# Where the first layer's gate rows are normalised: six of eight groups on GpSimd instead of ScalarE

## The reference, cut to what matters

```
x = x + attn_a(layernorm(x))     # arccos-kernel attention against 512 keys
x = x + ffn(layernorm(x))        # first layer: gate, top 2 of 8 experts, plus a shared expert
x = x + attn_b(layernorm(x))     # linear attention
x = x + ffn(layernorm(x))        # second layer
```

## Time and profile before

| what | us |
|---|---|
| median of 3 runs | 753.15 (751.16 to 757.9) |
| the profiled execution, its time | 754.43 |
| its span in the profile | 752.7 |
| mean granted TensorE clock, share of full speed | 0.89 |
| busy VectorE / TensorE / ScalarE / GpSimd | 551.8 / 523.5 / 425.5 / 379.0 |
| window 100 to 150 us: VectorE / ScalarE / GpSimd busy | 38.93 / 46.24 / 11.79 |
| window 150 to 200 us: VectorE / ScalarE / GpSimd busy | 37.98 / 28.34 / 23.06 |

### The profile page before, as it was taken

How to read it: one execution, slowest core, us unless ns; L and a number is a source line. 1 busy time by engine, 2 the same in 40 slices (tenths; PEclk the granted TensorE clock), 3 DMA queues, 4 the chain that set the end, 5 groups by cost and what they waited for, 6 DMA issues and landing times.

```text
span 752.7 us, 15794 instructions
## 1 busy us (share of the span) xinstructions
PE 523.5 (70%) x4441; PEld 376.2 (50%) x4442; DVE 551.8 (73%) x1219; ACT 425.5 (57%) x781; POOL 379.0 (50%) x374
## 2 busy tenths in 40 slices
PE   1376725564469949999993577764699689999940
PEld 0132225563224327788882466653244367888830
DVE  4987677888679818788882478875978377888835
ACT  1289988993446516566660468744455276666610
POOL 4032103233777744778875112246777426668760
PEclk9999969887689979999997689977699899999985
DMA  9600000000111313443432310000113134343319
GB/s 282 178 0 0 1 0 1 0 1 15 43 46 54 96 49 70 84 92 88 91 75 84 123 56 2 1 23 32 48 50 103 47 69 88 85 88 88 79 51 330
DMA packets 95049, 51.10 MB, mean 68 GB/s; under 512 B 76026, under 2 KB 84180, under 8 KB 94996
## 3 DMA queue, kind: packets, MB, share of 16 engines
q1 hardware_dynamic: 85908, 31.67, 17.3%
q0 software_dynamic: 9088, 18.76, 7.9%
HBM read 16.27 MB, written 23.90 MB: 53 GB/s over the span
## 4 chain that ended last, share of the span: by engine, by line
PE 36%; DVE 18%; POOL 14%; issue 14%; ACT 7%; DMA 6%; SPq 4%; POOLq 0%; DVEq 0%; ACTq 0%
POOL routed_rows L660 12%; PE PC L1218 6%; PE PC L1016 4%; PE PC L1220 4%; PE PC L1219 4%; PE PA L1202 3%; PE PA L1203 2%; PE PA L1204 2%; DMA big<-routed_rows 2%; DVE BN L1238 2%; SPq L526 2%; DMA RR<-expert_results 2%; PE PA L995 1%; DVE big L1443 1%; PE PB L1202 1%
## 5 line engine op out<-in xcount | busy, mean ns | idle before, releaser
L716 POOL DMA_INDIRECT expert_results<-RR,DG x156 | 176.2, 1130 | 96.3 <-DVE RR L1795 54.1
L660 POOL DMA_INDIRECT routed_rows<-big,SLQ x128 | 137.3, 1073 | 55.7 <-issue 44.8
L951 ACT ACTIVATE SC<-PA,B1T,scl 128x256 f32<-128x256 f32 x208 | 100.5, 564 | 77.3 <-PE PA L1204 77.3
L1218 PE MATMUL PC<-W2H,big 128*128 x624 | 118.4, 222 | 5.1 <-issue 3.0
L1219 PE MATMUL PC<-W2H,big 128*128 x624 | 116.7, 219 | 0.0
L1220 PE MATMUL PC<-W2L,big 128*128 x624 | 116.6, 219 | 0.0
L1786 DVE SCALAR_TENSOR_TENSOR big<-SC,scl,big 128x1024 f16<-128x1024 f32 x78 | 100.2, 1284 | 2.8
L1218 PEld LDWEIGHTS PC<-W2H,big 128*128 128x128 f16 x624 | 60.5, 97 | 26.8 <-issue 17.5
L1202 PE MATMUL PA<-big,W1H 128*128 128x256 f16 x208 | 59.1, 284 | 18.7 <-DMA big<-routed_rows 17.2
L1016 PE MATMUL PC<-QW,big 128*128 128x128 f32 x256 | 41.1, 336 | 42.6 <-DVE big L1443 27.9
L607 POOL TENSOR_TENSOR RS<-VA,halfneg 128x4 f32<-128x4 f32 x24 | 28.0, 1168 | 82.0 <-DVE VA L1477 81.9
(11 more groups left out here) (271 smaller groups left out, 1254.8 us busy)
## 6 DMA issues: line engine op xcount, KB each, us to landing
RR<-expert_results SPq DMA_DIRECT2D x16, 512.0 KB, 4.3
routed_rows<-pad_zeros SPq DMA_DIRECT2D x23, 128.0 KB
expert_results<-RR,DG POOLq DMA_INDIRECT x156
X<-n_L_attn_a_hidden_states SPq DMA_DIRECT2D x2, 1024.0 KB, 6.8
big<-in_L_ffn_w SPq DMA_DIRECT2D x1, 2048.0 KB, 8.9
routed_rows<-big,SLQ POOLq DMA_INDIRECT x128, 2.4
out_x<-X SPq DMA_DIRECT2D x8, 256.0 KB, 5.4
big<-routed_rows SPq DMA_TRANSPOSE x78
```

What stands on the lines that cost most here:

```text
L660: pool.indirect_dma_start(routed, bass.IndirectOffsetOnAxis(ap=SLQ[:, slot, t, c:c + 1], axis=0), XHL[:, slot, t, c, :].bitcast(I32), None ...
L716: pool.indirect_dma_start(results, bass.IndirectOffsetOnAxis(ap=DG[:, k, r, 0:1], axis=0), YT[:, k, r, :], None).then_inc(result_stored[k] ...
L951: ins = act.activation(HF[:, k % 3, b * RU:(b + 1) * RU], up_out(k, b), ACT.Gelu, scale=INV1, bias=B1T[:, bass.ds(b1_at + b, 1)])
L1218: pe.matmul(o, hh, W2H[:, at], start=(b == 0), stop=False)
```

## The change

For groups 0 to 5 of the first layer GpSimd makes the normalised rows: after the root of the group it computes (X - mean) times root for each of the four tiles. ScalarE's four instructions and VectorE's shift for these groups go. VectorE's `first_hi` waits for GpSimd's semaphore in place of ScalarE's. Groups 6 and 7, and the second layer, keep ScalarE's form, with the counts of their semaphores lowered by six.

```
+    POOLED = NG - 2
...
+            def normalise(g):
+
+                pool.wait_ge(s["root_made"], norm_turn[1, g] + 1)
+                wait(pool, s["xl_ready"], g - 1)
+                for t in range(TPG):
+                    at = g * TPG + t
+                    last = pool.tensor_scalar(XNG[:, g % 2, t, :], X[:, at, :], MV[:, at, 0:1], RS[:, at:at + 1],
+                                              ALU.subtract, ALU.mult)
+                last.then_inc(s["p_xn"], 1)
...
                     for g in range(NG - 2):
                         x_scale(g)
                         group_root(g, 1)
+                        normalise(g)
...
                     def first_normalise(g):
-                        gate_normalise(g)
+                        if g >= POOLED:
+                            gate_normalise(g)
                         if g == NG // 2 + 1:
                             gap(0)
...
                 def first_shift(g):
-                    shift(g, 1)
+                    if g >= POOLED:
+                        shift(g, 1)
 
                 def first_hi(g):
-                    dve.wait_ge(s["g_xn"], g + 1)
+                    if g < POOLED:
+                        dve.wait_ge(s["p_xn"], g + 1)
+                    else:
+                        dve.wait_ge(s["g_xn"], g - POOLED + 1)
```

More of the change, by code:

```diff
@@ L424, in build @@
             l_state l_kvm l_out l_nrm l_rnr l_ot l_fin ones_made stored
-            aggr_done eps_added root_made shift_made l_xn g_xn""".split()
+            aggr_done eps_added root_made shift_made l_xn g_xn p_xn""".split()
         s = {n: sem(n) for n in names}
@@ L865, in lin_normalise @@
                 def lin_normalise(g):
-                    act.wait_ge(s["shift_made"], norm_turn[2, g] + 1)
+                    act.wait_ge(s["shift_made"], norm_turn[2, g] - POOLED + 1)
                     wait(act, s["l_xt"], g - 1)
@@ L876, in gate_normalise @@
                 def gate_normalise(g):
-                    act.wait_ge(s["shift_made"], norm_turn[1 + 2 * layer, g] + 1)
+                    act.wait_ge(s["shift_made"], norm_turn[1 + 2 * layer, g] - POOLED + 1)
                     wait(act, s["xl_ready"], layer * NG + g - 1)
@@ L881, in gate_hi @@
                 def gate_hi(g):
-                    act.wait_ge(s["g_xn"], NG + g + 1)
+                    act.wait_ge(s["g_xn"], NG - POOLED + g + 1)
                     act.activation(XR[:, g * TPG:(g + 1) * TPG, 0:D], XNG[:, g % 2, :, :], ACT.Copy,
```

## The result

| | us |
|---|---|
| before, median of 15 runs | 755.11 (750.3 to 761.28) |
| changed, median of 15 runs | 763.58 (759.07 to 766.03) |
| ratio of changed to before | 1.0115, 95% interval 1.0092 to 1.0138 |

The changed kernel is slower by 1.15%, 8.5 us, outside the forecast range and beyond the 1% that was given a chance of 0.08. The profiled span is 763.3 us, where before's is 752.7.

The account below looks back on a forecast made before the run. No engine is busy throughout; the wait that ends last in the first stage counts. A net +1.2 us at the first scatter made 754.43 into 755.6 profiled; the median, 1.3 below, was forecast at 754.4 us, range 749.5 to 760.

Parts of the forecast that it names:

- rival 3: First stage: each GpSimd normalisation costs 1.0 us, mostly holding VectorE off; loop 12.8 us, +14.5, 769 us; chance 0.07.
- rival 2: TensorE's clock moves in the value groups: up to 6.8 us less or up to +5.6; chance 0.10 both directions together.
- The own price: One GpSimd 128x128 normalisation with two operands per partition: 0.3 to 0.35 us on an idle machine, 1.3 a group.
- the walk: First-stage timeline of GpSimd's queue: root, four normalisations, then scale and power for the next add_values; loop 9.9 to 10.0 us.
- T+7.3: T is the end of VectorE's moments; GpSimd's power for the next add_values was to be done 7.3 us later.
- Held off by VectorE: GpSimd waits until VectorE's running instruction ends; normalisations at T+1.5, T+2.2, T+3.6 and T+4.8, each between two of VectorE's.
- Delay to VectorE: Each GpSimd normalisation was taken to delay VectorE by 0.1 us; 0.4 instead would give about +5.
- The shift removed: Without shift(0) on VectorE, ninth(4) starts at 121.4 instead of 122.39; worth 0.9 to 1.0 us for value(2).
- The slow loops absorb the lateness: Where VectorE waits for logits after slow values, GpSimd's four ops fall in that wait; value(5) and value(6) 0.9 late.
- The sum: Net effect of the change at the first scatter: +1.2 us, passed on by what follows.
- Rival 1: GpSimd finds its gaps in the first stage and the relief counts: -1 to -2.2 us, 752 to 753; chance 0.27.

Follow-up runs that it names:

- with constants: Changed kernel with GpSimd's four normalising instructions using 0.25 and 1.5 in place of mean and root; first scale to first scatter 67.66 us, against 74.92 changed.
- extra work: Kernel before, with the four GpSimd normalising instructions added for groups 0 to 5, results unused; ratio to before 1.0144, first scale to first scatter 76.62 us.

## Why the prediction was wrong

The mechanism was the one forecast (add_values waits for a scale that is queued behind the normalisations); its size was not. The signs set down for rival 3 and rival 2 both came: single normalisations over 0.68 us with VectorE idle, and value times that are not where they were. Point by point:

- **The own price** is the step that failed. I put a normalisation at 0.33 us, from GpSimd's one-input forms of 0.29 and 0.41; it is 0.79. Those rows are of another kind of operation (both are selects), and even with constants the normalisation costs 0.64. In the walk the power was to be done at T+7.3 and was done at T+9.1 (141.43 to 150.56); 4 x (0.79 - 0.33) = 1.8 is the size of this difference. It is worked out, not run: no kernel had an own price of 0.33 together with the waits that come with operands. With constants (0.64 each, waits of 0.1 to 1.3 us a group) the way was 3.2 us over before's instead of 10.5. Of these 7.3 us the 0.15 between the prices makes 4 x 0.15 a loop, 3.0 in five; the rest goes with the waits, so they count for as much as the price.
- **Held off by VectorE**: the walk had about 3.5 us of waiting up to the scale; it is 3.25, all of it in front of the first two instructions. Right in sum, by luck, and wrong in form: I let each in between two of VectorE's, where the second misses two ends. Only the instructions with constants behave as I had walked it. The Trainium skill ("SBUF — State Buffer", section "SBUF: two separate sides") says that whichever starts first keeps the port pair for the whole instruction and the other fully blocks. The trace agrees that GpSimd waits for whole instructions of VectorE, and adds that it may wait for several; the other way round it does not agree, since the ninth at 143.66 took 1.23 us for 1.22 though a normalisation ran until 144.17.
- **Delay to VectorE**, 0.1 us each: 0.01 to 0.11 in the changed kernel. Right, as an upper value.
- **The shift removed**: value(2) came 123.43 - 114.01 = 9.42 us after the first scale, before 125.93 - 115.61 = 10.32. The 0.9 was right.
- **The slow loops absorb the lateness**: failed by the first point. A loop of 9.95 fits in one of 10.65; 11.81 does not, so nothing was absorbed and each group lost (1.0 and 1.3 us in these two). add_values(1) to (5) all waited for RX, where the forecast named (1) to (3). add_values(1), (3), (5) were late by 2.8, 8.0 and 10.3 us against the first scale, where I had +1.2, +2.3 and +0.9.
- **The sum**: the steps between adds were 8.28, 8.90, 9.46, 10.78 and 10.51 us before; they are 11.03 and then four of 11.8. That is 2.75 + 2.91 + 2.34 + 1.03 + 1.31 = 10.3, and 0.1 behind add_values(5), together the +10.5 of the way. The forecast had +1.2, +0.8 and +0.3 for the first three and took 1.4 back in the last two.
- **Rivals.** Rival 3 had the right place and nearly the right threshold: on its line between 0.33 us (loop 9.95) and 1.0 us (12.8), 0.79 gives 11.9. That the line comes so near is luck: it rested on VectorE being held off by 0.8 us an instruction, which did not occur. Its chance of 0.07 was too low: an operation with no row in the trace should have had the way up to the power's 1.04 more evenly. Rival 1's relief is 0.8 us, not 2.2. Rival 2, the clock: value(3) and value(6) did turn slower, as it allowed (5.30 and 6.28 for 3.84), but this plays no part in the changed kernel's loss, since every loop from add_values(1) on is 11.8 with values of 5.3 to 6.3 us; in the other versions slow groups stand where their gain was to be.
- ScalarE waited for value in every group but group 1, and no wait stood in front of ninth(4), nearly as said.

## What to carry to other kernels

Work moved to an idle engine is not free when that engine also holds a short step that a busy one waits for: put the short step (here the scale) ahead of the long one in the queue, or the busy engine may wait for the long one. Here this took the loss away and gave no gain. An operation that the trace does not show should be measured by itself before its queue is walked: between 0.33 and 0.79 us an instruction lay 1.8 us of every loop. And what an engine is relieved of counts only as far as the next bound, here the fp32 matmuls at the lower clock; 1.15% were lost here for a relief that was worth 0.8 us (0.1%) in its one profile.

## What the runs showed of the hardware

- GpSimd's tensor_scalar of two operations, 128x128 fp32: 0.64 us with constants, 0.71 with one operand per partition, 0.79 with two.
- Beside VectorE instructions with two SBUF inputs that follow each other without a gap, those with operands per partition waited for up to three of them (3.50 us in the changed kernel, 4.02 in that with extra work), those with constants for one (1.26).
- GpSimd's 128x512 instructions with two inputs took 1.08 to 1.37 us, one 1.90 behind a VectorE instruction that was still running; VectorE's instructions with two SBUF inputs that ran into them in groups 0 and 1 were 0.83 to 0.85 us longer. Beside the 128x128 ones it was 0.01 to 0.11 longer. So who waits, and how long, depends on the kind of instruction.
- The granted clock of the same 32 matmuls was 1.00 in some groups (3.84 us) and 0.55 in others (6.7 us), and 0.59 to 0.70 in those between (6.3 to 5.3 us, changed kernel). In two profiles of the kernel before the pattern was the same group by group; with a slightly different order of the other engines fast groups were slow, and which ones differed between two profiles.
